# Causal attention on one core: row maxima moved for both row groups at once, first pass six steps ahead, another order for GpSimd's stack lay-out

## The chip, the cores and the metric

The kernel runs on one core of a Trainium2 chip. Its time is the device time of one execution, in microseconds (us), the median of several runs. The core's engines are TensorE (PE in the profile, PEld for its weight loads), VectorE (DVE), ScalarE (ACT), GpSimd (POOL) and SyncE (SP), which here does nothing but issue DMAs.

## What is computed

The input x is 16 sequences of 1024 tokens by 256 features. Four layers follow each other, each as x = x + layer(layernorm(x)): a state-space layer, a feed-forward coupling network, attention, and the coupling network once more. The change is in the attention layer alone:

```python
x_proj = x @ Wqkv + bqkv
q = x_proj[:, :, :C].reshape(B, n_head, T, hd)
k = x_proj[:, :, C:2 * C].reshape(B, n_head, T, hd)
v = x_proj[:, :, 2 * C:].reshape(B, n_head, T, hd)
att = jnp.einsum('bhtd,bhsd->bhts', q, k) * (1.0 / jnp.sqrt(jnp.float32(hd)))
causal = jnp.tril(jnp.ones((T, T), dtype=bool))
att = jnp.where(causal, att, jnp.float32(-jnp.inf))
att = jax.nn.softmax(att, axis=-1)
y = att @ v
y = jnp.transpose(y, (0, 2, 1, 3)).reshape(B, T, C)
return y @ Wproj + bproj
```

Here B = 16, T = 1024, C = 256, n_head = 16 and hd = 16. The reshape has no transpose: head h is 64 neighbouring tokens, each of which holds 16 positions of that head. So a head has 1024 positions of 16 features, and there are 16 sequences x 16 heads.

## The kernel before

The attention phase takes the 16 sequences in turns b = 0..15. A turn has four slots q = 0..3, one for each group of four heads (a quad; quad number 4b + q). A slot has 20 steps (STEPS = 2 * UNITS2, UNITS2 = 10). In each step TensorE computes two things for two different quads, interleaved block by block:

- The second pass of the slot's own quad (second_piece, L1980, with its mask product L1928): scores key by query, with the row maxima subtracted inside the product. For this a 49th row of the query stack holds each query's maximum. ScalarE takes exp of the scores (exponentiate, L1839), and times_v (L2008) multiplies them by the values, at every odd step.
- The first pass of a later quad (first_piece, L1958): the plain scores, of which VectorE takes the row maxima (maxima, L1719 with the causal mask added, L1722 without). A quad has UNITS1 = 18 units of first pass, nine for each half p of the queries (PASS1). Units 1 and 8 of nine are one masked piece of 512 columns, units 3, 5 and 7 are two masked pieces (384 + 128, 256 + 256, 128 + 384), the others one plain piece of 512.

Both passes work on two row groups g (partitions 0 to 63 and 64 to 127): in a block, the second pass uses group g and the first pass group 1 - g, so that the two products run side by side in the array. A block below is one such pair; a step has two blocks. The first pass writes into three PSUM banks in rotation (first_wait, semaphore s1_free): a block may start when VectorE has finished with what the third-last first-pass block wrote. The second pass has three banks likewise (second_wait, exp_done).

The first pass runs LEAD = 4 steps ahead (first_pass_at): in a slot, steps 0 to 13 do units 4 to 17 of the next quad, steps 14 and 15 have no first pass, and steps 16 to 19 do units 0 to 3 of the quad after it. The prologue does all 18 units of quad 0 and LEAD units of quad 1.

When a half's nine units are done (step 4 for p = 0, step 13 for p = 1), VectorE reduces the maxima to row_max (L1727), waits on max_moved for the buffer, and transposes them into row_max_T (L1733). SyncE then moves them with eight small DMAs (move_max, L1417) into the 49th row of the query stack: tasks at steps 6 and 15 of its slot. TensorE waits for the moves of half p at step p of the next slot (L1970).

Beside the two passes, one side task on TensorE stands at every even step from 2 to 16 (x_events): finished heads turned back (L2050), the output turned and projected (L2057, L2065), and the input of a later half sequence turned (L2032) and projected to q and k (L2036) and to v (L2042). Each uses the one bank x_ps. In slot 3, the two turned pieces of x ("project" 0 and 1) come at PE steps 4 and 8 and the first projection of them at step 10. Between them stand a copy by ScalarE (project, L1849) and a split into a high and a low part by GpSimd (split, L1541 and L1543); TensorE waits for the second split (split_done) before the projection at step 10.

GpSimd also lays out the stacks of quad + 3: lay_out (L1553, L1555) copies each of the two staged tiles, queries and keys, into its stack in two pieces, at task times LAY_OUT_AT = 6.3, 7.6, 10.2, 12.2. The first piece of a side waits for its staged loads (L1397, twelve DMAs of 128 KB, issued at a slot's start).

Every engine runs its tasks in the order of these step numbers (in_order sorts them, ties in the order in which they were added).

## Time and profile before

| | |
|---|---|
| median of 3 runs | 3927.08 us (3926.39 to 3935.58) |
| span of the profiled execution | 3930.1 us |
| PE busy, share of the span | 3667.3 us, 93% |
| DVE busy | 2960.1 us, 75% |
| ACT busy | 2237.0 us, 57% |
| POOL busy | 1663.9 us, 42% |
| the four steady slots of one turn (1923.9 to 2063.9) | 140.0 us |

The profile lists no device time of its own for the profiled execution; its span, from first to last instruction, is 3.0 us above the median and inside the range of the runs. Attention's steps begin near 1077 us and end near 3303 us; what stands before and after them are the other three layers.

The span is cut by time (windows), by who waited for whom (waits), and by single instructions (timeline). A row of the timeline gives start, duration, engine, line, operation, output and inputs, shapes, how many were merged, and in brackets the idle time of the engine before it and what ended it. SyncE's rows are the time in which it issued.

### The profile page before, as it was taken

How to read it: one execution, taken by the hardware profiler on the slowest of the kernel's cores; microseconds unless marked ns; L12 is line 12 of the kernel's file. 1: busy time of each engine (PE TensorE's matmuls, PEld its weight loads, DVE VectorE, ACT ScalarE, POOL GpSimd, SP SyncE). 2: the span in 40 equal slices, each digit the busy share in tenths (PEclk: the TensorE clock that was granted, in tenths of full speed). 3: DMA queues.
4: the chain of work that ended last, by engine and by line, in shares of the span. 5: the costliest groups of instructions: out<-in, count | busy, mean ns of one | idle time of the engine just before them, and what ended most of it. 6: DMA issues, size and time to landing. Idle time of an engine off the chain costs nothing. (4 is left out here: it accounts for less than half of the span.)

```text
span 3930.1 us, 77952 instructions
## 1 busy us (share of the span) xinstructions
PE 3667.3 (93%) x26062; PEld 2353.8 (60%) x26062; DVE 2960.1 (75%) x9275; ACT 2237.0 (57%) x4407; POOL 1663.9 (42%) x2027
## 2 busy tenths in 40 slices
PE   6998999998689999999999999999999997999997
...
GB/s 71 102 101 103 43 65 65 46 57 35 158 112 114 112 117 107 121 109 115 123 108 116 117 112 118 105 126 104 117 122 110 101 71 61 34 69 60 65 39 49
DMA packets 701469, 361.31 MB, mean 92 GB/s; under 512 B 305072, under 2 KB 668080, under 8 KB 701104
## 3 DMA queue, kind: packets, MB, share of 16 engines
q1 hardware_dynamic: 701104, 356.65, 50.8%
...
## 5 line engine op out<-in xcount | busy, mean ns | idle before, releaser
L1839 ACT ACTIVATE att_probs<-att_s 128x512 f32<-128x512 f32 (+1 forms) x2560 | 1319.3, 557 | 755.3 <-PE att_s L1928 430.9
L1719 DVE CUSTOM_DVE_ANT_0 att_s<-att_s,att_above 128x384 f32<-128x384 f32 (+3 forms) x2048 | 958.0, 514 | 189.0 <-PE att_s L1958 188.9
L1980 PE MATMUL att_s<-att_qs,att_ks 49*128 49x512 f32 (+3 forms) x3072 | 917.9, 388 | 90.0 <-ACT att_probs L1839 29.1
L1958 PE MATMUL att_s<-att_ks,att_qs 48*128 48x512 f32 (+3 forms) x3072 | 964.2, 407 | 5.8 <-DVE att_maxima L1722 3.7
L1980 PEld LDWEIGHTS att_s<-att_qs,att_ks 49*128 49x128 f32 x3072 | 459.7, 185 | 650.9 <-ACT att_probs L1839 433.6
L1722 DVE TENSOR_REDUCE att_maxima<-att_s 128x1 f32<-128x512 f32 x1024 | 668.8, 682 | 225.6 <-PE att_s L1958 219.3
L2008 PE MATMUL att_o_ps<-att_probs,att_vs 128*32 128x512 f32 (+3 forms) x6144 | 632.1, 499 | 0.5 <-ACT att_probs L1839 0.5
L1958 PEld LDWEIGHTS att_s<-att_ks,att_qs 48*128 48x128 f32 x3072 | 487.6, 188 | 25.1 <-DVE att_maxima L1719 8.0
L1097 PE MATMUL ffn_h2p<-ffn_h,ffn_w 128*128 128x512 f32 x768 | 363.3, 595 | 3.0 <-ACT ffn_h L968 0.9
L1928 PE MATMUL att_s<-att_mask,att_places 64*128 64x64 bf16 (+1 forms) x3072 | 332.5, 205 | 0.0
L1719 DVE DVE_READ_ACCUMULATOR2_ANT att_maxima<- 128x1 f32 x2048 | 290.0, 142 | 0.0
L946 ACT ACTIVATE ffn_uv<-ffn_uvp 128x512 f32<-128x512 f32 x256 | 153.1, 598 | 238.1 <-PE ffn_uvp L1072 238.1
L1612 POOL TENSOR_TENSOR att_x_res<-att_x_res,att_bp_row 128x512 f32<-128x512 f32 x60 | 76.2, 1285 | 420.6 <-DMA att_x_res<-x 419.7
L1555 POOL CAST att_qs<-att_staged 113x1024 fp32r<-113x1024 f32 x128 | 251.9, 1991 | 0.0
L976 ACT ACTIVATE ffn_h<-ffn_turned,ffn_b 128x512 f32<-128x512 f32 x384 | 241.9, 683 | 13.5 <-PE ffn_turned L1088 11.6
L1555 POOL CAST att_ks<-att_staged 113x1024 fp32r<-113x1024 f32 x126 | 249.4, 1992 | 0.0
L968 ACT ACTIVATE ffn_h<-ffn_h2p,ffn_b 128x512 f32<-128x512 f32 x192 | 131.9, 687 | 196.1 <-PE ffn_h2p L1097 196.1
L2008 PEld LDWEIGHTS att_o_ps<-att_probs,att_vs 128*32 128x32 f32 x6144 | 134.2, 108 | 161.1 <-issue 121.7
L1088 PEld LDWEIGHTS ffn_turned<-identf,ffn_uv 128*128 128x128 f32 x1536 | 174.5, 142 | 75.6 <-issue 53.9
L2036 PE MATMUL att_x_ps<-att_xnT,att_wqkv 128*128 128x512 f32 x714 | 198.0, 413 | 17.5 <-POOL att_xnT L1543 17.5
L158 ACT ACTIVATE ssm_xnT<-ssm_turned 128x512 fp32r<-128x512 f32 x64 | 34.9, 595 | 313.2 <-PE ssm_turned L166 313.2
L1088 PE MATMUL ffn_turned<-identf,ffn_uv 128*128 128x128 f32 x1536 | 201.6, 274 | 10.3 <-DVE ffn_uv L823 8.0
...
## 6 DMA issues: line engine op xcount, KB each, us to landing
...
qk_scratch<-att_parts SPq DMA_DIRECT2D x128, 512.0 KB, 3.7
...
```

Source lines behind the costliest of these rows:

```text
L976: last = a(h1[k][:, f, :], turned_ps[:, f, :], ACT.Gelu, bias=b1[:, f:f + 1])
L1088: last = pe.transpose(turned_ps[:, f, t * P:(t + 1) * P], of[:, t, f * P:(f + 1) * P], identf[:, :])
L1097: last = mm(h2_ps[:, :], w2[:, f, :], h1[k][:, f, :], start=(f == 0), stop=(f == KT - 1))
L1555: last = g.tensor_copy(stack[0:ROWS, :].rearrange("p (t c) -> p t c", c=HD)[:, e * n:(e + 1) * n, :], staged[side][0:ROWS, :, e * n:(e + 1 ...
L1719: last = v.tensor_tensor_reduce(scores, scores, above[:, CH - w:CH], 1.0, -3.0e38, ALU.add, ALU.max, to)
L1722: last = v.tensor_reduce(to, scores, AX.X, ALU.max)
L1839: a(probs[u % 2][2 * g + p][:, 0:n], bank[:, 0:n], ACT.Exp).then_inc(exp_done, 1)
L1928: last = mm(blocks[:, at, GROUP * half:GROUP * (half + 1)], places[rows, 2 * (1 - k) + half, :], mask[rows, 1 - k, 0:len(cols), :], start= ...
L1958: last = mm(bank[:, col:col + w], rows_of(qs[buf], g, KROWS, p, BT * blk, BT * (blk + 1)), rows_of(ks[buf], g, KROWS, p, t0, t1), start=k ...
L1980: last = mm(bank[:, col:col + w], rows_of(ks[buf], g, SHIFT + 1, p, BT * j, BT * (j + 1)), rows_of(qs[buf], g, SHIFT + 1, p, t0, t1), star ...
L2008: last = mm(o_ps[32 * i:32 * i + 32, HD * (t0 - first_t):HD * (t1 - first_t)], vs[s][:, NBLK * head + j, :], probs[u % 2][i][:, col:col + ...
L2036: last = mm(bank[:, :], wq[i][:, f, cols], xnT[k][:, f, :], start=(n == 0), stop=(n == KT * len(PARTS_R) - 1))
```

## The change

Three things change:

1. move_max issues four DMAs instead of eight: each takes the eight blocks of both row groups (16 partitions of row_max_T) and writes two partitions of the query stack, instead of 8 partitions into one. Bytes and the number of 128-byte pieces stay; the waits on max_moved count 64 instead of 128 for each quad. SyncE's two tasks stand at steps 4 and 13 instead of 6 and 15.
2. LEAD is 6 instead of 4. Steps 0 to 11 do units 6 to 17 of the next quad, steps 12 and 13 have no first pass, steps 14 to 19 do units 0 to 5 of the quad after it. The row maxima are reduced at steps 2 and 11 instead of 4 and 13. The prologue does six units of quad 1 instead of four.
3. In slot 3 alone, GpSimd's lay-out tasks stand at 9.2, 9.4, 11.2 and 13.2 instead of 6.3, 7.6, 10.2 and 12.2.

```diff
--- before.py
+++ after.py
@@ -1221,9 +1221,10 @@
     FIRST_U2, LAST_U2 = (0, 3), (2, 9)
     UNITS1, UNITS2 = 2 * len(PASS1), len(PASS2)
     STEPS = 2 * UNITS2
-    LEAD = 4
+    LEAD = 6
     EVACUATE_AT = (7, 1)
-    LAY_OUT_AT, PREPARE_AT, PIECES = (6.3, 7.6, 10.2, 12.2), 6, 2
+    LAY_OUT_AT, LAY_OUT_BEHIND_X_AT = (6.3, 7.6, 10.2, 12.2), (9.2, 9.4, 11.2, 13.2)
+    PREPARE_AT, PIECES = 6, 2
     NORMALISE_AT = (14.4, 15.5, 16.5, 17.5)
 
     X_PROLOGUE = 22
@@ -1411,11 +1412,10 @@
 
                 def move_max(quad, buf, p):
                     sp.wait_ge(row_max_turned, 2 * quad + p + 1)
-                    for g in range(2):
-                        to = qs[buf][GROUP * g + SHIFT:GROUP * g + SHIFT + 1, NBLK * P * p:NBLK * P * (p + 1)].bitcast(F32)
-                        for a in range(4):
-                            sp.dma_start(to.rearrange("o (n a r) -> o n a r", a=4, r=32)[:, :, a, :],
-                                         row_max_T[p][32 * a + NBLK * g:32 * a + NBLK * (g + 1), :]).then_inc(max_moved[p], 16)
+                    to = qs[buf][SHIFT:SHIFT + GROUP + 1:GROUP, NBLK * P * p:NBLK * P * (p + 1)].bitcast(F32)
+                    for a in range(4):
+                        sp.dma_start(to.rearrange("g (n a r) -> g n a r", a=4, r=32)[:, :, a, :],
+                                     row_max_T[p][32 * a:32 * a + 2 * NBLK, :]).then_inc(max_moved[p], 16)
 
                 def load_res(b, r):
                     k = r % 2
@@ -1435,8 +1435,8 @@
                                            (4 * b + 5, 2 * b + 2, 0, 1), (4 * b + 6, 2 * b + 3, 1, 0))[q]
                         tasks += [(side, lambda side=side: load_stack(quad, hb, s, qq, side)) for side in range(2)]
                     if more or q < 3:
-                        tasks += [(6, lambda: move_max(4 * b + q + 1, (q + 1) % 4, 0)),
-                                  (15, lambda: move_max(4 * b + q + 1, (q + 1) % 4, 1))]
+                        tasks += [(4, lambda: move_max(4 * b + q + 1, (q + 1) % 4, 0)),
+                                  (13, lambda: move_max(4 * b + q + 1, (q + 1) % 4, 1))]
                     if q == 0:
                         if not first:
                             tasks += [(2, lambda r=r: load_res(b - 1, r)) for r in range(2)]
@@ -1630,7 +1630,7 @@
                     if more or q == 0:
                         for side in range(2):
                             for e in range(PIECES):
-                                tasks += [(LAY_OUT_AT[PIECES * side + e],
+                                tasks += [((LAY_OUT_BEHIND_X_AT if q == 3 else LAY_OUT_AT)[PIECES * side + e],
                                            lambda side=side, e=e: lay_out(quad + 3, side, e, not first or q > 0))]
                     in_order(tasks)
 
@@ -1728,7 +1728,7 @@
                                         maxima_of[p][:, :, :, :].rearrange("p g n e -> p (g n) e"),
                                         AX.X, ALU.max).then_inc(row_max_ready, 1)
                         if not isinstance(quad, int) or quad > 0:
-                            dve.wait_ge(max_moved[p], 128 * quad)
+                            dve.wait_ge(max_moved[p], 64 * quad)
                         dve.wait_ge(row_max_ready, 2 * quad + p + 1)
                         v.transpose(row_max_T[p][:, :], row_max[p][:, :].bitcast(F32)).then_inc(row_max_turned, 1)
 
@@ -1967,7 +1967,7 @@
                         before = 3 if use >= 3 else (1, 4, 4)[use]
                         pe.wait_ge(exp_done, 2 * STEPS * quad + 2 * step + g - before + 1)
                     if step < 2 and g == 0:
-                        pe.wait_ge(max_moved[step % 2], 128 * (quad + 1))
+                        pe.wait_ge(max_moved[step % 2], 64 * (quad + 1))
 
                 def second_piece(buf, step, g, k):
```

How this moves rows on three engines, where the prediction speaks of them:

VectorE in a slot 1, from the maxima of step 2 to the first unit behind the row maximum. RECIPROCAL and the TENSOR_TENSOR after it are the division of the turned heads; row_max is L1727. Before:

```order
L1722 TENSOR_REDUCE att_maxima0<-att_s1_0 128x1
L1722 TENSOR_REDUCE att_maxima0<-att_s1_1 128x1
L1741 RECIPROCAL att_recip<-att_x_ps 128x16
L1744 TENSOR_TENSOR att_y<-att_x_ps,att_recip 128x8x32
L1719 ISA att_s1_2,att_maxima0<-att_s1_2,att_above 128x128
L1719 ISA att_maxima0 128x1
...
L1719 ISA att_s1_2,att_maxima0<-att_s1_2,att_above 128x512
L1719 ISA att_maxima0 128x1
L1727 TENSOR_REDUCE att_row_max0<-att_maxima0 128x16
L1733 STREAM_TRANSPOSE att_row_max_T0<-att_row_max0 128x32
L1722 TENSOR_REDUCE att_maxima1<-att_s1_0 128x1
```

After:

```order
L1722 TENSOR_REDUCE att_maxima0<-att_s1_0 128x1
L1722 TENSOR_REDUCE att_maxima0<-att_s1_1 128x1
L1719 ISA att_s1_2,att_maxima0<-att_s1_2,att_above 128x128
L1719 ISA att_maxima0 128x1
...
L1719 ISA att_s1_2,att_maxima0<-att_s1_2,att_above 128x512
L1719 ISA att_maxima0 128x1
L1727 TENSOR_REDUCE att_row_max0<-att_maxima0 128x16
L1733 STREAM_TRANSPOSE att_row_max_T0<-att_row_max0 128x32
L1741 RECIPROCAL att_recip<-att_x_ps 128x16
L1744 TENSOR_TENSOR att_y<-att_x_ps,att_recip 128x8x32
L1722 TENSOR_REDUCE att_maxima1<-att_s1_0 128x1
```

The row maximum and its transpose come two units earlier, ahead of the division of the heads, and the plain unit that followed the division at step 4 now follows it at step 3.

GpSimd in a slot 3, from the split of the first turned piece on (full and xnT are the splits of the turned input, qs and ks the stacks, parts the splits of the projections). Before:

```order
L1541 CAST att_xnT0<-att_full0 128x512
L1543 TENSOR_TENSOR att_xnT1<-att_full0,att_xnT0 128x512
L1553 TENSOR_TENSOR att_pool_carrier<-att_eps 1x1
L1555 CAST att_qs2<-att_staged0 113x1024 x2
L1541 CAST att_xnT0<-att_full1 128x512
L1543 TENSOR_TENSOR att_xnT1<-att_full1,att_xnT0 128x512
L1553 TENSOR_TENSOR att_pool_carrier<-att_eps 1x1
L1555 CAST att_ks2<-att_staged1 113x1024
L1541 CAST att_parts<-att_full2 128x512
L1543 TENSOR_TENSOR att_parts<-att_full2,att_parts 128x512
L1555 CAST att_ks2<-att_staged1 113x1024
```

After:

```order
L1541 CAST att_xnT0<-att_full0 128x512
L1543 TENSOR_TENSOR att_xnT1<-att_full0,att_xnT0 128x512
L1541 CAST att_xnT0<-att_full1 128x512
L1543 TENSOR_TENSOR att_xnT1<-att_full1,att_xnT0 128x512
L1553 TENSOR_TENSOR att_pool_carrier<-att_eps 1x1
L1555 CAST att_qs2<-att_staged0 113x1024 x2
L1541 CAST att_parts<-att_full2 128x512
L1543 TENSOR_TENSOR att_parts<-att_full2,att_parts 128x512
L1553 TENSOR_TENSOR att_pool_carrier<-att_eps 1x1
L1555 CAST att_ks2<-att_staged1 113x1024
L1541 CAST att_parts<-att_full0 128x512
```

The second split of the turned input now stands directly behind the first, and each lay-out piece moved behind one more split.

TensorE at the end of a slot, second block of step 17 and both blocks of step 18 (s2 is the second pass, s1 the first). Before:

```order
L1980 MATMUL att_s2_1<-att_qs2,att_ks2 128x384
L1958 MATMUL att_s1_0<-att_ks0,att_qs0 128x512
L1980 MATMUL att_s2_1<-att_qs2,att_ks2 128x128
L1928 MATMUL att_s2_1<-att_mask,att_places 128x2x64 x2
L1980 MATMUL att_s2_2<-att_qs2,att_ks2 128x256
L1928 MATMUL att_s2_2<-att_mask,att_places 128x64 x2
L1958 MATMUL att_s1_1<-att_ks0,att_qs0 128x512
L1980 MATMUL att_s2_0<-att_qs2,att_ks2 128x256
L1928 MATMUL att_s2_0<-att_mask,att_places 128x64 x2
L1958 MATMUL att_s1_2<-att_ks0,att_qs0 128x512
```

After:

```order
L1980 MATMUL att_s2_1<-att_qs2,att_ks2 128x384
L1958 MATMUL att_s1_1<-att_ks0,att_qs0 128x384
L1980 MATMUL att_s2_1<-att_qs2,att_ks2 128x128
L1928 MATMUL att_s2_1<-att_mask,att_places 128x2x64 x2
L1958 MATMUL att_s1_1<-att_ks0,att_qs0 128x128
L1980 MATMUL att_s2_2<-att_qs2,att_ks2 128x256
L1928 MATMUL att_s2_2<-att_mask,att_places 128x64 x2
L1958 MATMUL att_s1_2<-att_ks0,att_qs0 128x512
L1980 MATMUL att_s2_0<-att_qs2,att_ks2 128x256
L1928 MATMUL att_s2_0<-att_mask,att_places 128x64 x2
L1958 MATMUL att_s1_0<-att_ks0,att_qs0 128x512
```

The block in which the first pass had one piece of 512 columns now has two, 384 and 128, with the second behind the masks of the other pass.

## Rows read from the trace of the kernel before

**Rows 1.** The page's third part, DMA: packets, MB, share of 16 engines.

```profile
q1 hardware_dynamic: 701104, 356.65, 50.8%
```

**Rows 2.** Windows: length; PE, PEld, DVE, ACT, POOL busy (instructions); clock; DMA share; GB/s.

```profile
1923.90:2063.90 140.00, 134.31 (x1156) 78.41 (x1155) 111.97 (x374) 93.85 (x189) 77.12 (x68) 1.00 0.76 114
1958.80:1991.10 32.30, 31.58 (x284) 18.24 (x282) 27.57 (x91) 22.73 (x47) 14.45 (x12) 1.00 0.63 84
```

**Rows 3.** Waits of PE, 1100 to 3230: us in total, times, longest us.

```profile
PE att_s L1980 <- ACT att_probs L1839: 25.5, 65, 0.4
PE att_s L1980 <- DVE att_maxima L1722: 24.9, 35, 1.1
PE att_x_ps L2036 <- POOL att_xnT L1543: 17.5, 14, 1.8
PE att_s L1980 <- DVE att_maxima L1719: 16.0, 49, 0.3
```

**Rows 4.** Timeline of two slots 3: ScalarE's copy, GpSimd's second split, the projection.

```profile
1760.90 0.60 ACT L1849 ACTIVATE att_full<-att_x_ps 128x512 f32<-128x512 f32 x1
1762.37 0.60 POOL L1541 CAST att_xnT<-att_full 128x512 fp32r<-128x512 f32 x1
1764.46 0.71 PE L2036 MATMUL att_x_ps<-att_xnT,att_wqkv 128*128 128x512 f32 x2 [1.79 <-POOL att_xnT L1543]
...
2041.37 0.61 ACT L1849 ACTIVATE att_full<-att_x_ps 128x512 f32<-128x512 f32 x1
2042.04 0.61 POOL L1541 CAST att_xnT<-att_full 128x512 fp32r<-128x512 f32 x1
2042.73 1.27 POOL L1543 TENSOR_TENSOR att_xnT<-att_full,att_xnT 128x512 fp32r<-128x512 f32 x1
2044.14 1.61 PE L2036 MATMUL att_x_ps<-att_xnT,att_wqkv 128*128 128x512 f32 x6 [1.02 <-POOL att_xnT L1543]
```

**Rows 5.** Timeline of SP and PE at the first steps, and two windows there.

```profile
1058.36 5.59 SPq L1417 DMA_DIRECT2D att_qs<-att_row_max_T  x8
1064.05 5.96 SPq L1397 DMA_DIRECT2D att_staged<-qk_scratch  x12
1076.50 6.43 SPq L1417 DMA_DIRECT2D att_qs<-att_row_max_T  x8
1088.29 0.79 PE L1980 MATMUL att_s<-att_qs,att_ks 49*128 49x512 f32 x1 [10.02 <-DMA att_qs<-att_row_max_T]
1058.00:1064.00 6.00, 4.39 (x12) 1.87 (x11) 4.58 (x12) 1.97 (x2) 0.00 (x0) 0.78 0.01 1
1064.00:1087.00 23.00, 13.96 (x34) 7.48 (x33) 15.14 (x53) 1.19 (x2) 7.82 (x6) 0.50 1.15 191
```

**Rows 6.** Waits of PE, 3230 to 3303, the one on a move.

```profile
PE att_s L1980 <- DMA att_qs<-att_row_max_T: 0.7, 1, 0.7
```

**Rows 7.** Timeline of DVE and PE at the end of a slot 1.

```profile
1987.79 0.70 DVE L1719 CUSTOM_DVE_ANT_0 att_s<-att_s,att_above 128x512 f32<-128x512 f32 x1 [0.49 <-PE att_s L1958]
1988.70 0.35 PE L1980 MATMUL att_s<-att_qs,att_ks 49*128 49x256 f32 x1 [0.33 <-DVE att_maxima L1719]
1990.68 0.57 DVE L1719 CUSTOM_DVE_ANT_0 att_s<-att_s,att_above 128x384 f32<-128x384 f32 x1 [0.21 <-PE att_s L1958]
1991.70 0.47 PE L1980 MATMUL att_s<-att_qs,att_ks 49*128 49x512 f32 x1 [0.39 <-ACT att_probs L1839]
```

**Rows 8.** Timeline of DVE in a slot 1, steps 3 to 5, and PE's first block of step 5.

```profile
1963.70 0.29 DVE L1719 CUSTOM_DVE_ANT_0 att_s<-att_s,att_above 128x128 f32<-128x128 f32 x1
1965.21 0.73 DVE L1719 CUSTOM_DVE_ANT_0 att_s<-att_s,att_above 128x512 f32<-128x512 f32 x1
1967.11 1.25 DVE L1722 TENSOR_REDUCE att_maxima<-att_s 128x1 f32<-128x512 f32 x2
1965.56 0.29 PE L1980 MATMUL att_s<-att_qs,att_ks 49*128 49x256 f32 x1
```

**Rows 9.** Window with a lowered clock near the end of attention.

```profile
3190.00:3203.70 13.70, 13.70 (x50) 6.94 (x50) 6.31 (x25) 4.97 (x10) 10.35 (x8) 0.50 0.68 76
```

## The prediction

> **What bounds the kernel now.** I read the windows first, then TensorE's waits, then the timeline around each wait. In a steady turn of 140.0 us TensorE is busy 134.31 us, VectorE 111.97 and ScalarE 93.85, at the full clock [rows 2]. So TensorE sets the pace, and a change pays only where it shortens one of its idle pieces. They are few: from 1100 to 3230 it waits 25.5 us for ScalarE, 24.9 and 16.0 us for VectorE's maxima and 17.5 us for GpSimd's split, 83.9 us in all [rows 3]. No wait for a moved row maximum is among them; such waits stand only at the two ends, 10.02 us in the first slot and 0.7 us in the last [rows 5, 6]. VectorE is the second to watch: in a slot 1 it is busy 27.57 of 32.30 us [rows 2], and nearly all of its idle time falls where there is no first pass.
>
> **Part 1, the order on GpSimd.** The wait for the split occurs once in a turn, in slot 3. At 2042.04 the split starts 0.06 us after the end of ScalarE's copy (2041.37 + 0.61 = 2041.98), and yet TensorE waits 1.02 us [rows 4]: the wait is made of the copy's time and of the split's own 0.61 and 1.27 us, and no order on GpSimd shortens that. At 1762.37 the copy had ended at 1761.50, the lay-out held GpSimd for 0.87 us, and TensorE waited 1.79 us [rows 4]. So what the new order can give is the part over 1.02 us: 17.5 - 14 x 1.02 = 3.2 us over the 14 waits [rows 3, 4]. It costs nothing: what is laid out late is first read a slot later, and the later splits have two full steps each.
>
> **Part 2, the row maxima in four DMAs.** SyncE issues eight in 5.59 us [rows 5]; four should take half. In steady slots no one waits for them: worth nothing. In the prologue they stand on the path. SyncE issues the first half's moves from 1058.36, then the loads of quad 2's stacks from 1064.05, then stores, then the second half's moves from 1076.50, and TensorE resumes at 1088.29. From 1058 to 1064 the DMA engines are at 0.01 of their time, from 1064 to 1087 they are full [rows 5]. So the end of the queue is set by when the heavy transfers start, and this is earlier by half of 5.59: 2.8 us. TensorE would in that case resume at 1085.5. The two added units of quad 1 run inside this wait: at VectorE's 1.25 us for a plain unit [rows 8], and somewhat more for a masked one, they take some 3 us of the 10.02. The last slot's 0.7 us [rows 6] goes as well, since its moves start two steps earlier and are shorter, and the two units that the loop no longer holds save about 0.6 us at the end (estimate: two steps of unpaired blocks beside two of paired ones). Sum: 4.1 us, all gain; from below zero gain if the queue is full anyway, to 5.6 us if both moves count.
>
> The Trainium skill, DMA: Bandwidth & Descriptors, section "Why a DMA increments its semaphore by 16 and not by 1", says that a DMA from SP's queue runs on as many engines as divide the slowest dimensions of both its sides, 16 at most. The old moves (8 partitions to one of 8 blocks) would run on 8 engines, the new ones (16 partitions to two) on 2, with 32 pieces each instead of 8. The rule speaks against the change; no view here shows a packet's engine. At the mean packet time of the page, 0.508 x 3930.1 x 16 / 701104 = 0.046 us [rows 1], it would make 1.1 us more until a move has landed, as an estimate, and the prologue's gain would be 1.7 instead of 2.8 us.
>
> **Part 3, LEAD 6.** The work is the same; what changes is which first-pass unit stands beside which step. Two places matter.
>
> *End of a slot.* Steps 18 and 0 have no side task, so blocks follow each other with nothing between them, and the block at step 19 must wait for VectorE's maximum of the block at the end of step 17, three blocks back. Before, this is one masked piece of 512: VectorE starts at 1987.79 and TensorE resumes at 1988.70, 0.91 us on, after an idle 0.33 [rows 7]. It now becomes unit 3, pieces of 384 and 128, as the one at 1990.68, from which TensorE resumes at 1991.70, 1.02 us on [rows 7]: 0.11 us more. Besides, its second piece is issued behind the other pass's piece of 128 and its masks, where the single 512 was issued first; this costs between 0 and 0.14 us more, and I take the middle, 0.07. So 0.18 us in each of 61 slots: 11.0 us (6.7 to 15.3). The wait at step 1 (0.39 us, put down to ScalarE, but VectorE's unit ends 0.15 us before it) keeps its size, since 256 + 256 takes VectorE as long as 384 + 128.
>
> *Start of a slot.* The masked unit 8 and the row maximum move from step 4 to step 2, where a plain unit stood. From 1965.21 to 1967.11 they take 1.90 us, a plain unit 1.25 [rows 8]. So VectorE is 0.65 us further behind at step 3, and the division of the heads now follows this too. Before, unit 7 starts at 1963.70 in a slot 1; now unit 9 starts near 1964.4, its second half ends near 1965.73, and TensorE's first block of step 5, which stood at 1965.56 [rows 8], must wait for it and some 0.14 us of signalling (the distance from VectorE's end to TensorE's start, as 0.15 at 1991.70), to 1965.87: 0.3 us. From then the two orders have given VectorE the same work. Slots 1 and 3 (small side tasks at steps 2 and 4) pay this: 30 x 0.28 = 8.4 us. In slots 0 and 2 the side task of step 4 is the long one, and VectorE recovers before it matters: 0.05 x 31 = 1.6 us. The bounds for both together are 0 and 0.65 x 30 = 19.5 us.
>
> *Pairing.* The unpaired steps 12 and 13 carry no masks of the second pass, 14 and 15 did; the masks now run beside a first-pass block. I take 0.05 us gained per slot, 3 us (0 to 6).
>
> **Sum.** On the profiled execution's 3930.1 us: -3.2 - 4.1 + 11.0 + 8.4 + 1.6 - 3.0 = +10.7 us. The median of the runs lies 3.0 us below this span, so 3927.1 + 10.7 = 3937.8 us; I say 3937.
>
> **Rivals.**
>
> *The longer waits for VectorE do not come (A, chance 0.20).* If the block at step 19 and the ones at step 5 wait no longer than before, only -3.2 - 4.1 and half of the pairing, -1.5, remain: 3927.1 - 8.8 = 3918. For it: VectorE has idle time before step 17's maximum (0.49 us before 1987.79 [rows 7]). Against it: the wait there is latency, not backlog, and VectorE's idle time does not shorten it.
>
> *The whole wait for GpSimd goes (B, chance 0.13).* If the changed phases also bring ScalarE's copy 1 us ahead of TensorE, all 17.5 us go, with 4.1 and 3: 3927.1 - 24.6 = 3902.5. Against it: the split starts 0.06 us behind the copy in the undisturbed case [rows 4], and nothing moves the copy.
>
> *VectorE becomes the bound (C, chance 0.22), slower.* Its price is the whole of the moved row maximum in slots 1 and 3, 19.5 us, and the upper end at step 19, 15.3 us: with 1.6, and less 3.2, 4.1 and 3.0, +26.1, which is 3953. It decides from the point where VectorE's backlog at step 4 exceeds the slack of three banks; by the rows it exceeds it by 0.3 us in slots 1 and 3, and C holds if nothing of it is recovered.
>
> *The clock (D, chance 0.07).* From 3190.00 to 3203.70 TensorE had only 0.50 of its clock while busy throughout [rows 9]; half of 13.7 us, 6.9 us, is lost there, and it could go or come a second time with another arrangement near the end: 3930 or 3944 about the forecast.
>
> *The moves are hidden anyway.* For the steady slots this is my forecast, and if the queue in the prologue is full regardless, 2.8 us less gain gives 3940; it is part of the forecast's own range.
>
> **How the numbers follow.** The forecast itself has a chance of 0.38, with a range of its own from 3930 to 3945. The bound of what a measurement can tell is 0.3%, 11.8 us: faster is below 3915.3, slower above 3938.9. Faster: B whole and 0.04 of A, 0.17. Slower: C whole, 0.11 of the forecast and 0.02 of D, 0.35. The rest, 0.48, is within. The range from 3908 to 3955 holds the forecast, A, D, the upper third of B and, since its middle lies at 3953, somewhat over half of C; it leaves out 0.18.
>
> **What would show each step.** Right: the wait on the split counts 15 or 14 times with 1.0 us each, longest about 1.1; the first slot's wait on the moves ends near 1085.5, and no move is waited for in the last; the idle before step 19's first block reads about 0.5 instead of 0.33 in every slot; a new wait of 0.2 to 0.3 us for VectorE's maxima at step 5 in slots 1 and 3; a turn of four slots of about 141 us instead of 140.0. Wrong: a turn of under 139.6 us, which would say that the first pass further ahead gave TensorE time that I don't see; waits on moved maxima in steady slots, if four DMAs land later than eight; or the idle before step 19 unchanged at 0.33.

## The result, and the profile after

The changed kernel takes 3964.91 us (median, 3954.92 to 3968.43) against 3928.19 us of the kernel before in the same comparison (3926.39 to 3937.59). The ratio is 1.008, with a 95% interval from 1.0066 to 1.0094: slower by 31 us by the ratio and 37 by the medians. The prediction said 3937 us and at most 3955.

First the page's line on DMA and two windows of the kernel after, a steady turn and its slot 1 (columns as in [rows 2]):

```profile
q1 hardware_dynamic: 693936, 356.62, 50.0%
...
1932.60:2074.15 141.55, 134.66 (x1156) 79.19 (x1155) 112.78 (x374) 94.00 (x189) 77.02 (x68) 1.00 0.74 113
1967.87:2000.66 32.79, 31.67 (x283) 18.39 (x282) 27.77 (x91) 22.76 (x48) 14.39 (x12) 1.00 0.83 104
```

The turn is 1.55 us longer than in [rows 2], with the same instructions on every engine and the clock at 1.00. That is the steady loss. TensorE's waits from 1100 to 3266 (us in total, times, longest) answer to [rows 3]:

```profile
PE att_s L1980 <- DVE att_maxima L1719: 33.0, 63, 0.6
PE att_s L1980 <- ACT att_probs L1839: 28.6, 67, 0.5
PE att_s L1980 <- DVE att_maxima L1722: 27.2, 35, 1.1
PE att_x_ps L2036 <- POOL att_xnT L1543: 13.2, 14, 0.9
PE att_s L1928 <- issue: 2.9, 2, 2.5
PE att_s L1980 <- issue: 1.6, 1, 1.6
```

The wait for masked maxima (L1719) has doubled, from 16.0 to 33.0 us. The wait for GpSimd's split has fallen from 17.5 to 13.2 us, and is 0.9 us each time. The last two rows are waits put down to "issue": TensorE had nothing it waited for, and its next instruction came late. The kernel before has one such wait in this stretch, 1.4 us, at full clock; the changed kernel has four, of 1.6, 2.5, 0.6 and 0.4 us (the row of the one of 0.6 us is not shown). Where the two long ones stand is seen in the timeline. The windows of lowered clock are below them; the first and the third come with these two waits, the second does not:

```profile
1720.33 0.44 PE L1980 MATMUL att_s<-att_qs,att_ks 49*128 49x384 f32 x1 [1.59 <-issue]
2581.54 0.21 PE L1928 MATMUL att_s<-att_mask,att_places 64*128 64x64 bf16 x1 [2.54 <-issue]
...
1720.70:1724.20 3.50, 3.50 (x15) 2.17 (x11) 1.45 (x3) 0.87 (x2) 0.00 (x0) 0.51 1.51 110
2499.00:2512.60 13.60, 13.60 (x80) 9.08 (x78) 7.57 (x24) 5.37 (x11) 0.00 (x0) 0.50 1.23 126
2580.90:2587.70 6.80, 6.16 (x28) 3.53 (x31) 2.06 (x5) 1.62 (x4) 0.72 (x2) 0.50 1.04 81
```

In each of the three windows TensorE has 0.50 of its clock (the level of 1.2 GHz) while busy nearly throughout. The kernel before had none between 1097.6 and 3159.3.

What such an instruction waited for is most likely its own fetching. The third part of the page has a DMA queue for instructions (here of the kernel before: packets, MB, share of 16 engines):

```profile
q8 instruction: 204, 3.34, 0.4%
```

These are packets of 16 KB. In all 17 profiles together TensorE has 25 waits of over 1 us put down to issue between 1100 and 3300, and each of the 25 ends 1.2 to 2.0 us after the end of such a packet, of which one comes only about every 14.6 us.

The prologue and the first slot answer to [rows 5], the end of a slot 1 to [rows 7]:

```profile
1057.44 2.33 SPq L1417 DMA_DIRECT2D att_qs<-att_row_max_T  x4
1059.87 5.74 SPq L1398 DMA_DIRECT2D att_staged<-qk_scratch  x12
1072.42 2.15 SPq L1417 DMA_DIRECT2D att_qs<-att_row_max_T  x4
1081.97 0.79 PE L1980 MATMUL att_s<-att_qs,att_ks 49*128 49x512 f32 x1 [1.51 <-DMA att_qs<-att_row_max_T]
...
1997.34 0.57 DVE L1719 CUSTOM_DVE_ANT_0 att_s<-att_s,att_above 128x384 f32<-128x384 f32 x1 [0.54 <-PE att_s L1958]
1997.82 0.33 DVE L1719 CUSTOM_DVE_ANT_0 att_s<-att_s,att_above 128x128 f32<-128x128 f32 x1
1998.36 0.35 PE L1980 MATMUL att_s<-att_qs,att_ks 49*128 49x256 f32 x1 [0.61 <-DVE att_maxima L1719]
```

TensorE waits 1.51 us for the moves instead of 10.02 us, in part because it comes to this wait later: VectorE and TensorE do two more units ahead of the loop. At step 19 it waits 0.61 instead of 0.33 us.

**Where the 36.2 us between the two profiled spans lie.** I cut attention into turns, from the start of the first exponential of a turn to that of the next. Before, turn 0 begins at 1077.6 and turn 1 at 1223.9; after, at 1079.8 and 1220.5: -3.4 us. Turns 1 to 13 take 1819.8 before and 1857.8 after: +38.1. The last two take 258.9 and 260.1: +1.2. The rest gives +0.3. The shortest turn, which nothing disturbs, is 139.65 before and 141.55 after, so 13 x 1.90 = 24.7 us of the 38.1 are steady. What turns 1 to 13 take beyond 13 times the shortest was 4.3 us and is now 17.6: 13.3 us for late instructions and lowered clock.

Where in a turn the steady part lies, I read from the starts of TensorE's blocks of the second pass, counted from the first one of their slot (medians over turns 2 to 12, us more than in the kernel before):

| stretch | slot 0 | slot 1 | slot 2 | slot 3 | a turn |
|---|---|---|---|---|---|
| steps 0 to 5 | 0.04 | 0.30 | 0.02 | 0.30 | 0.66 |
| steps 6 to 11 | 0.25 | 0.08 | 0.28 | 0.06 | 0.67 |
| steps 12 to 16 | -0.12 | -0.12 | -0.15 | -0.14 | -0.53 |
| steps 17 and 18 | 0.12 | 0.01 | 0.00 | 0.01 | 0.14 |
| the wait at step 19 | 0.15 | 0.28 | 0.27 | 0.27 | 0.97 |

The second run of the changed kernel (e17) and LEAD 6 alone (e1) give the same sums to within 0.05. The whole kernels are compared by the two numbers above, the shortest turn and what turns 1 to 13 take beyond it:

| kernel | shortest turn | turns 1 to 13 beyond 13 of these | at half clock, 1100 to 3240 | time against before |
|---|---|---|---|---|
| before | 139.65 | 4.3 | 17.1 | |
| changed | 141.55 | 17.6 | 30.7 | 1.0080 |
| changed, second run (e17) | 141.56 | 13.9 | 13.7 | 1.0097 |
| LEAD 6 alone (e1) | 141.54 | 12.7 | 30.7 | 1.0093 |
| all but LEAD (e2) | 139.60 | 5.9 | 6.8 | 0.9979 |
| order on GpSimd alone (e6) | 139.60 | 3.0 | 0.0 | 0.9977 |
| four DMAs alone (e15) | 139.67 | 13.3 | 13.6 | 0.9998 |
| changed, row maximum later (e4) | 140.90 | 21.8 | 37.5 | 1.0091 |
| changed, plain unit at 17 (e16) | 140.03 | 12.7 | 27.3 | 1.0001 |
| changed, both (e9) | 139.56 | 4.2 | 6.8 | 0.9996 |
| changed, plain at odd places (e3) | 141.16 | 46.1 | 105.9 | 1.0136 |
| LEAD 5 (e11) | 141.55 | 42.9 | 81.9 | 1.0126 |
| before, plain at odd places (e5) | 140.67 | 11.8 | 6.9 | 1.0098 |
| same with the other two parts (e7) | 140.62 | 17.1 | 34.1 | 1.0064 |
| before, copy of 192 (e10) | 140.30 | 8.7 | 6.8 | 1.0024 |
| before, copy of 320 (e12) | 140.63 | 7.5 | 23.8 | 1.0031 |
| LEAD 4, plain at 17 (e13) | 139.54 | 5.4 | 6.8 | 0.9977 |

### The profile page after: what moved, and what is told of

It reads as the page before. It is cut to its first block and busy times, and to the rows that moved or that the text cites. A ratio compares the mean times of both kernels' runs of the same rounds, so it can differ in the third digit from the quotient of the medians.

```text
span 3966.3 us, 77436 instructions
## 1 busy us (share of the span) xinstructions
PE 3689.6 (93%) x26062; PEld 2373.5 (60%) x26062; DVE 2972.0 (75%) x9275; ACT 2241.4 (57%) x4407; POOL 1663.0 (42%) x2027
## 5 line engine op out<-in xcount | busy, mean ns | idle before, releaser
L1719 DVE CUSTOM_DVE_ANT_0 att_s<-att_s,att_above 128x384 f32<-128x384 f32 (+3 forms) x2048 | 958.4, 516 | 156.2 <-PE att_s L1958 154.1
L1980 PE MATMUL att_s<-att_qs,att_ks 49*128 49x512 f32 (+3 forms) x3072 | 928.9, 391 | 106.5 <-DVE att_maxima L1719 34.0
L1958 PE MATMUL att_s<-att_ks,att_qs 48*128 48x512 f32 (+3 forms) x3072 | 990.4, 410 | 6.7 <-DVE att_maxima L1722 4.4
L1980 PEld LDWEIGHTS att_s<-att_qs,att_ks 49*128 49x128 f32 x3072 | 470.3, 186 | 675.9 <-ACT att_probs L1839 435.8
L1722 DVE TENSOR_REDUCE att_maxima<-att_s 128x1 f32<-128x512 f32 x1024 | 677.9, 685 | 258.4 <-PE att_s L1958 256.0
L1928 PE MATMUL att_s<-att_mask,att_places 64*128 64x64 bf16 (+1 forms) x3072 | 361.2, 206 | 2.9 <-issue 2.9
L1719 DVE DVE_READ_ACCUMULATOR2_ANT att_maxima<- 128x1 f32 x2048 | 290.7, 142 | 0.0
L2036 PE MATMUL att_x_ps<-att_xnT,att_wqkv 128*128 128x512 f32 x714 | 200.6, 417 | 13.8 <-POOL att_xnT L1543 13.2
```

Source lines behind the costliest of these rows:

```text
L1719: last = v.tensor_tensor_reduce(scores, scores, above[:, CH - w:CH], 1.0, -3.0e38, ALU.add, ALU.max, to)
L1722: last = v.tensor_reduce(to, scores, AX.X, ALU.max)
L1928: last = mm(blocks[:, at, GROUP * half:GROUP * (half + 1)], places[rows, 2 * (1 - k) + half, :], mask[rows, 1 - k, 0:len(cols), :], start= ...
L1958: last = mm(bank[:, col:col + w], rows_of(qs[buf], g, KROWS, p, BT * blk, BT * (blk + 1)), rows_of(ks[buf], g, KROWS, p, t0, t1), start=k ...
L1980: last = mm(bank[:, col:col + w], rows_of(ks[buf], g, SHIFT + 1, p, BT * j, BT * (j + 1)), rows_of(qs[buf], g, SHIFT + 1, p, t0, t1), star ...
L2036: last = mm(bank[:, :], wq[i][:, f, cols], xnT[k][:, f, :], start=(n == 0), stop=(n == KT * len(PARTS_R) - 1))
```

## The experiments

### Which part loses: LEAD alone, and everything but LEAD

```diff
-    LEAD = 4
+    LEAD = 6
```

> The kernel before with LEAD 6 and nothing else (eight moves of a row maximum, at steps 6 and 15; the old order on GpSimd). Theory T: the loss comes from the first pass being six slots ahead, which makes TensorE wait longer for VectorE at step 19 and at steps 4 and 5 (in the profiles 0.61 instead of 0.33 us a slot, and 0.35 us in slots 1 and 3), and it brings the stretches at the lower clock too. Then this kernel loses as much as the changed one and does not get the gains of the other two parts: about 3965 + 3 (layout) + 3 to 5 (moves) = 3968 to 3975 us, TensorE's wait for the maxima about 33 us in all from 1080 to 3270. Rival U: the pairing makes only the steady 20 us or so, and the other half of the loss, the short stretches at half clock with their idle pieces ahead, belongs to the moves in four DMAs or to the new order on GpSimd. Then this kernel stands at 3945 to 3955 us and its profile shows the clock at 1.00 from 1100 to 3150.

Measured: 3969.71 us, ratio 1.0093 (1.0077 to 1.011). Its waits from 1100 to 3266:

```profile
PE att_s L1980 <- DVE att_maxima L1719: 32.9, 63, 0.6
PE att_s L1980 <- ACT att_probs L1839: 28.7, 67, 0.5
PE att_s L1980 <- DVE att_maxima L1722: 26.8, 36, 1.1
```

These are the changed kernel's, and so are the shortest turn and the half clock. Theory T holds: LEAD makes the whole loss, and the two other parts were not needed for the stretches at half clock.

The counterpart is the changed kernel with

```diff
-    LEAD = 6
+    LEAD = 4
-                        tasks += [(4, lambda: move_max(4 * b + q + 1, (q + 1) % 4, 0)),
-                                  (13, lambda: move_max(4 * b + q + 1, (q + 1) % 4, 1))]
+                        tasks += [(6, lambda: move_max(4 * b + q + 1, (q + 1) % 4, 0)),
+                                  (15, lambda: move_max(4 * b + q + 1, (q + 1) % 4, 1))]
```

> The changed kernel with LEAD back at 4 and the moves back at steps 6 and 15: what remains of the change is the order on GpSimd and four DMAs instead of eight. Theory T: -3.2 us from the waits for the split (14 at 0.94 to 1.02 us instead of 17.5 us in all) and -3 to -5 us from the prologue and the end: 3920 to 3924 us, no stretch of half clock that the kernel before does not have. Rival U (these two parts bring the stretches at half clock): 3930 to 3945 us.

Measured: 3921.58 us against 3932.07, ratio 0.9979 (0.9968 to 0.9989). The other two parts together gain some 8 us, as T said. Against T, the profile has a stretch of 6.8 us at half clock (at 1854.7) where the kernel before has none; it follows an instruction that came 2.4 us late.

### The two small parts by themselves

The order on GpSimd alone (LAY_OUT_BEHIND_X_AT in the kernel before):

> The kernel before with the new order on GpSimd and nothing else. Theory T: the 14 waits for the split of slot 3 fall from 17.5 us in all to 14 x 1.0 us and nothing else changes: 3 us less than before, 3924 to 3930 us, the slot 3 at 35.7 us in every turn instead of 35.7 to 36.5. Rival U (this part has a cost of its own elsewhere on GpSimd's queue): the same waits, but the time at or above that of before.

Measured: 3913.80 us against 3922.82, ratio 0.9977 (0.9967 to 0.9987). All ten runs lie between 3912.97 and 3916.12; those of before are spread from 3915.10 to 3932.67. The wait it was made for reads

```profile
PE att_x_ps L2037 <- POOL att_xnT L1544: 14.2, 14, 1.0
```

and has lost 3.3 us, as expected. The time has lost 9 us. What part of the rest may be is seen in the kernels that keep the old order. In the one with four DMAs alone, two of TensorE's waits for the split reach 2.3 us, and the clock is at half behind each:

```profile
1337.38 2.90 PE L2035 MATMUL att_x_ps<-att_xnT,att_wqkv 128*128 128x512 f32 x6 [2.30 <-POOL att_xnT L1542]
2599.73 1.64 PE L2035 MATMUL att_x_ps<-att_xnT,att_wqkv 128*128 128x512 f32 x4 [2.35 <-POOL att_xnT L1542]
...
1337.30:1340.70 3.40, 3.32 (x9) 2.32 (x11) 0.00 (x0) 0.00 (x0) 2.01 (x2) 0.50 0.00 0
2600.20:2603.60 3.40, 3.40 (x14) 1.92 (x17) 0.58 (x3) 0.62 (x2) 1.45 (x1) 0.50 0.00 0
```

Each of these slots is 2.8 us longer than its like (38.5 instead of 35.72 us), 1.3 us by the longer wait and the rest by the clock. In the four kernels run with the old order and LEAD 4 there are nine waits for the split of 2.0 to 2.4 us, and five have half clock behind them (the profile of the kernel before itself has none above 1.8 us); in the kernels with the new order the longest is 1.1 us, and none has. The two stretches of [rows 9] and at 3159.3, 17.1 us in all, are gone as well in this one profile: the last two turns take 252.0 instead of 258.9 us. That the new order caused this is not shown, since the waits ahead of them (0.67 and 0.66 us) are there with full clock too. Nor is the narrow spread explained: it did not come with the same order in the kernels with four DMAs (3912.78 to 3931.45 and 3903.22 to 3922.92).

Four DMAs instead of eight, alone:

> The kernel before with a row maximum's moves in four DMAs instead of eight and nothing else. Theory T: 3 to 6 us less, all of it ahead of the first slot and in it, as the wait on the moves there falls from 10.0 to about 4 us; a steady turn as before. Rival (the moves land later when each is one transfer of twice as many pieces, or SyncE was not what held the stacks up): within 1 us of before, or slower.

Measured: 3919.95 us against 3919.25, ratio 0.9998 (0.9984 to 1.0012). In the profile the gain is there:

```profile
1053.97 2.34 SPq L1416 DMA_DIRECT2D att_qs<-att_row_max_T  x4
1069.12 2.87 SPq L1416 DMA_DIRECT2D att_qs<-att_row_max_T  x4
1079.56 0.79 PE L1979 MATMUL att_s<-att_qs,att_ks 49*128 49x512 f32 x1 [5.09 <-DMA att_qs<-att_row_max_T]
```

The wait on the moves is 5.09 instead of 10.02 us and turn 0 takes 142.38 instead of 146.27 us, so 3.9 us as theory T had it; the interval of the times, -6 to +5 us, is too wide to show it. The time from SyncE's last issue to TensorE's start is 1079.56 - 1071.99 = 7.6 us, where it was 1088.29 - 1082.93 = 5.4 us [rows 5], so some of what SyncE saves in issuing (12.0 us of issuing before, 5.2 now) is waited for all the same. By the rule that the Trainium skill, DMA: Bandwidth & Descriptors, gives in its section "Why a DMA increments its semaphore by 16 and not by 1", the new moves run on 2 engines instead of 8. The 2.2 us are of the sign that this gives and twice the 1.1 us that the prediction estimated from it, but they may as well be the stores ahead of them in the queue; no run here tells the two apart.

### What at LEAD 6 costs: the two-piece units and the row maximum

The changed kernel with two of the first pass's units changed about, so that step 17 has a plain unit (one piece of 512, no masks) in place of 384 + 128. PASS1 holds for both halves of the queries, so the same exchange also puts a plain unit at step 6, where the second half has its 384 + 128:

```diff
-    PASS1 = [[(7, 0, 32)], [(7, 32, 64)], [(6, 0, 32)], [(6, 32, 56), (0, 0, 8)], [(5, 0, 32)],
+    PASS1 = [[(7, 0, 32)], [(7, 32, 64)], [(6, 32, 56), (0, 0, 8)], [(6, 0, 32)], [(5, 0, 32)],
              [(5, 32, 48), (1, 0, 16)], [(4, 0, 32)], [(4, 32, 40), (2, 0, 24)], [(3, 0, 32)]]
```

> The changed kernel with only the two units changed about that put a plain one at step 17 (the row maximum stays at step 2). Steady part, from the run with both edits (turn 139.6 us) and the one with the later row maximum alone (141.0): the unit is worth 1.3 us a turn, the turn here 140.25 us. Theory T (the half-clock stretches of the changed kernel come where the wait of 0.6 us and the next of 0.42 us stand close together, at the ends of slot 3, and with the missing instructions in slot 2): none at the ends of slot 3, 3928 to 3940 us. Rival V (they come with LEAD 6 and the later row maximum removed them by chance): 20 us or more of half clock between 1100 and 3240 us, 3940 to 3955 us.

Measured: 3930.34 us against 3929.49, ratio 1.0001 (0.9986 to 1.0015). Waits from 1100 to 3230:

```profile
PE att_s L1980 <- ACT att_probs L1839: 41.1, 112, 0.9
PE att_s L1980 <- DVE att_maxima L1722: 26.2, 35, 1.1
PE att_x_ps L2036 <- POOL att_xnT L1543: 15.1, 14, 1.1
PE att_x_ps L2036 <- issue: 1.9, 1, 1.9
```

The row for L1719 has gone; ScalarE ends the wait at step 19 now:

```profile
1990.63 0.35 PE L1980 MATMUL att_s<-att_qs,att_ks 49*128 49x256 f32 x1 [0.27 <-ACT att_probs L1839]
```

The turn falls from 141.55 to 140.03 us. By the stretches of the table above, 1.22 us of this come at step 19, where the wait is now below that of the kernel before (0.27 instead of 0.33 us), and 0.45 us in steps 6 to 11; the others lose 0.12. Nearly all of the loss in the time is gone with this one exchange. Against rival V the time is 39.6 us below that of the changed kernel on the same chip (3969.90); but V is right that 20 us or more of half clock stay (27.3 us), none of it at the ends of slots 3. Of the 39 us between the two spans (3966.8 and 3927.8), 1.52 x 13 = 19.8 us lie in turns 1 to 13 as their steady part, some 8 us in the last two turns (260.0 to 251.9), 6.1 us ahead of attention's steps and 5.5 us behind them, where the two kernels are the same. So by the profiles 1.52 x 15 = 23 us are the exchange's steady part, and nothing here ties the rest to it.

The other suspect, the row maximum one unit later:

```diff
-                    if unit % len(PASS1) == len(PASS1) - 1:
+                    if unit in (len(PASS1), UNITS1 - 1):
+                        p = unit // len(PASS1) if unit == UNITS1 - 1 else 0
```

> The changed kernel, where VectorE reduces the row maximum of the first row group one unit later (behind the unit of step 3 instead of step 2), so that step 2 carries 0.65 us less of VectorE's work. Theory T (the wait at steps 4 and 5 in slots 1 and 3 is VectorE's backlog from this reduction at step 2): the wait goes where it is only a matter of order, 0.2 to 0.35 us in 30 slots, 6 to 10 us: 3955 to 3959 us. Rival U: the backlog is the sum of units 8 and 9 with the division of the heads, wherever the reduction stands: the time is 3963 to 3968 us and the steps 4 and 5 take as long as in the changed kernel.

Measured: 3964.25 us, ratio 1.0091 (1.0062 to 1.012). In the time, no gain; in the profile, exactly the expected one. A steady slot 1 takes 32.49 instead of 32.79 us, and from the first to the second block of step 5 it is 0.34 instead of 0.58 us (the changed kernel's two rows first, then this kernel's):

```profile
1974.35 0.38 PE L1980 MATMUL att_s<-att_qs,att_ks 49*128 49x256 f32 x1
1974.93 0.35 PE L1980 MATMUL att_s<-att_qs,att_ks 49*128 49x256 f32 x1
```

```profile
1978.58:2011.07 32.49, 31.45 (x283) 18.32 (x281) 27.71 (x91) 22.77 (x47) 14.45 (x12) 1.00 0.81 102
...
1985.12 0.38 PE L1981 MATMUL att_s<-att_qs,att_ks 49*128 49x256 f32 x1
1985.46 0.28 PE L1981 MATMUL att_s<-att_qs,att_ks 49*128 49x256 f32 x1
```

The shortest turn is 0.65 us less; over 13 turns 8.5 us. They were given back: the first slot waits 5.4 us for the moves (1.5 in the changed kernel's profile), and turns 1 to 13 hold 4.2 us more of late instructions and half clock than the changed kernel. Both edits together:

> The changed kernel with only two of the first pass's units per row group changed about, so that a plain unit of one piece of 512 stands at step 17, while steps 8 and 19 keep theirs, and with the first row maximum one unit later. Theory T (steady part: the two-piece unit at step 17 makes the 0.61 us wait at step 19; and what is left over the kernel before is the lower clock that follows such waits): the wait at step 19 falls to about 0.3 us, slots 1 and 3 lose another 0.3 us (as the run with the later row maximum alone showed, 32.81 to 32.48 us), the turn comes to about 140.1 us, the pair of waits 0.6 and 0.42 us at the end of slot 3 is gone and no 13.6 us stretch of half clock follows there: 3930 to 3942 us. Rival V (the pairing costs elsewhere, or the stretches at half clock come with LEAD 6 whatever stands at step 17): 3950 to 3970 us.

Measured: 3922.03 us against 3922.82, ratio 0.9996 (0.9985 to 1.0007). The turn is

```profile
1922.10:2061.66 139.56, 133.81 (x1155) 78.29 (x1155) 112.68 (x374) 94.24 (x188) 76.94 (x68) 1.00 0.75 115
```

that of the kernel before in its best turns, with the first pass six slots ahead. So the distance costs nothing by itself: 1.52 us of each turn's 1.99 go with the exchanged units (step 19 and steps 6 to 11), 0.47 with the place of the row maximum (0.65 where the other edit is not there). Theory T expected 140.1 us for the turn: it had not counted that the exchange also helps in steps 6 to 11 and leaves a shorter wait at step 19 than the kernel before has.

### The same exchange carried further, and LEAD 5

First I had changed about more than that: in the changed kernel, plain one-piece units at all odd places.

```diff
-    PASS1 = [[(7, 0, 32)], [(7, 32, 64)], [(6, 0, 32)], [(6, 32, 56), (0, 0, 8)], [(5, 0, 32)],
-             [(5, 32, 48), (1, 0, 16)], [(4, 0, 32)], [(4, 32, 40), (2, 0, 24)], [(3, 0, 32)]]
+    PASS1 = [[(7, 32, 64)], [(7, 0, 32)], [(6, 32, 56), (0, 0, 8)], [(6, 0, 32)], [(5, 32, 48), (1, 0, 16)],
+             [(5, 0, 32)], [(4, 32, 40), (2, 0, 24)], [(4, 0, 32)], [(3, 0, 32)]]
```

> The changed kernel with the units of each row group of the first pass in another order: the plain one-piece unit and its two-piece neighbour change places, so that at step 17 a plain unit of one piece of 512 stands where 384 + 128 stood, at 19 likewise, and step 16 and 18 carry the two-piece ones. The work is the same. Theory T (the wait at step 19 is made by the unit whose maxima VectorE takes there): the idle before step 19 falls from 0.61 to 0.33 us or less in each of 61 slots, 17 us or more, and the other steps change by a few us in either direction: 3940 to 3950 us. Rival U (the pairing is minor): within 5 us of the changed kernel's 3965.

Measured: 3987.82 us, ratio 1.0136 (1.0087 to 1.0186). Both theories missed. The wait at step 19 fell to 0.27 us, but this order also puts a masked two-piece unit at step 7, where VectorE is already behind with the statistics of x, and TensorE waits for its maxima at the second block of step 8 and the first of step 9 in slots 0 and 2. Two rows and the window behind them:

```profile
2390.41 0.47 PE L1980 MATMUL att_s<-att_qs,att_ks 49*128 49x512 f32 x1 [0.98 <-DVE att_maxima L1719]
2391.17 0.46 PE L1980 MATMUL att_s<-att_qs,att_ks 49*128 49x512 f32 x1 [0.26 <-DVE att_maxima L1719]
...
2392.10:2398.90 6.80, 6.80 (x31) 2.60 (x24) 3.62 (x13) 3.09 (x6) 6.80 (x7) 0.50 0.89 125
```

Of 27 such pairs, 15 are followed by 3.4 to 10.2 us at half clock; the slot of the pair shown takes 3.0 us more than its like (38.7 instead of 35.75). In the kernel before and in the changed one, the same place has waits of mostly 0.80 to 0.85 and 0.1 us, and, between 1100 and 3200, no half clock behind them. LEAD 5, with the moves at 5 and 14 and the old order of the units, meets the same at step 7:

> The changed kernel with LEAD 5 instead of 6, and the moves one step later, at 5 and 14. At step 17 stands unit 2, plain, in one piece of 512, and the row maximum comes at step 3. Theory T (what costs is the unit at step 17 and the row maximum at step 2, not the distance as such): the wait at step 19 is 0.33 us or less, slots 1 and 3 lose little at steps 4 and 5, the turn is 139.5 to 140.5 us: 3915 to 3935 us. Rival V (the distance itself costs, each slot of lead about half of what six cost over four): 3940 to 3950 us.

Measured: 3973.71 us against 3922.82, ratio 1.0126 (1.0105 to 1.0146). The wait at step 19 is 0.12 to 0.17 us, as T said, but the time is far above both of the forecast ranges and the worst but one: 0.97 and 0.26 us at step 8, eight times followed by half clock, and besides a new wait of 8.9 us in all for the additions of the residual (L1752), which at step 12 now stand beside the last unit and the second row maximum. At a slot's end it gains, in its middle it loses.

Is it LEAD after all? The same order of units at LEAD 4, first on the kernel before, then with the other two parts:

> The kernel before (LEAD 4, old layout, eight moves) with the units of the first pass changed about in the same way as in the run of the changed kernel that became slower: plain one-piece units at the odd places, so that a plain unit stands at step 8 too. Theory T (what costs is which unit stands at step 8 and at step 17, not the distance of the two passes): the wait behind step 8 rises from about 0.95 to 1.25 us in slots 0 and 2, stretches of 3.4 to 10.3 us at half clock follow it in a third of the cases or more, and the time is 3945 to 3990 us although the wait at step 19 is gone. Rival W (half clock comes with a first pass further ahead than four): no such stretches, 3910 to 3925 us.

> LEAD 4, new order on GpSimd, four DMAs, and plain one-piece units at all odd places, so that one stands at step 8. The waits there read 0.95 to 1.0 and 0.26 us in slots 0 and 2; the steady turn is 140.6 us, about 1.0 us above that of the kernel with only the unit at step 17 changed. Theory T (at LEAD 4 these waits only cost themselves; what the same order lost on the kernel before beyond its turns came from the long waits for GpSimd): 3922 to 3935 us. Rival U (the waits at step 8 lower the clock in some executions at LEAD 4 as well): 3940 to 3960 us.

Measured: 3956.82 us against 3919.25, ratio 1.0098 (1.0067 to 1.013), and 3955.29 us against 3929.49, ratio 1.0064 (1.004 to 1.0087). So T's time was right for the first, though not the half clock that it expected, and rival U's for the second. The unit at step 7 costs at LEAD 4 as well: 1.0 us a turn by its waits (140.67 and 140.62 instead of 139.6), 15 us of the 25 to 37. In the second kernel 2 such pairs of waits (0.94 and 0.26 us) are followed by 10 us at half clock, in the first none in the one profile, which was its fastest run (3939.24 of 3939.24 to 3965.49). So the lowered clock follows nearly the same pair of waits in 15, 8, 2 and 0 cases of some 27 at LEAD 6, 5, 4 and 4, each counted in one profile.

### A longer wait at step 19 without LEAD 6

To separate the wait from the order, I put a copy by VectorE between the arrival of step 17's last block and its maximum, in the kernel before:

```diff
                         dve.wait_ge(s1_full, n + 2 - g)
+                        if g == 0 and unit == 1 and (not isinstance(quad, int) or quad > 0):
+                            v.tensor_copy(delay[:, :], above[:, 0:192])
```

> The kernel before with one added operation of VectorE in each slot, a copy of 128 x 192 between the arrival of the last block of step 17 and its maximum: its order, its moves and its units are as before, and only the latency for which the block at step 19 waits grows by the copy, some 0.2 to 0.3 us. Theory T (a longer wait at this place costs its own length, and brings stretches at half clock behind it): the wait at step 19 reads about 0.55 to 0.65 us, the steady turn is 0.8 to 1.2 us longer, and one to three stretches of 3.4 to 13.6 us at half clock appear between 1100 and 3150: 3945 to 3965 us. Rival W (the lower clock has to do with LEAD 6 otherwise): the turn longer by as much, the clock at 1.00 from 1100 to 3150: 3940 to 3946 us.

> As the run with the added copy of VectorE in each slot of the kernel before, with 128 x 320 instead of 128 x 192 (0.26 us there): about 0.39 us. The wait at step 19 should read 0.60 to 0.65 us, as in the changed kernel. Theory T (a wait as long as this, followed by the 0.42 us one at the end of slot 3, lets the clock fall there in some turns): one to three stretches of 13 us at half clock at the ends of slots 3, steady turn 140.8 us: 3945 to 3960 us. Rival W (waits only cost themselves): the turn 1.2 us longer over 15 turns, 3938 to 3945 us, and full clock from 1100 to 3150.

Measured: 3931.52 us against 3922.82, ratio 1.0024 (1.0012 to 1.0035), and 3933.49 us against 3919.25, ratio 1.0031 (1.0016 to 1.0045). The wider copy reproduces the waits of the changed kernel at the end of a slot 3:

```profile
2063.67 0.35 PE L1983 MATMUL att_s<-att_qs,att_ks 49*128 49x256 f32 x1 [0.58 <-DVE att_maxima L1722]
2066.04 0.50 PE L1983 MATMUL att_s<-att_qs,att_ks 49*128 49x512 f32 x1 [0.42 <-ACT att_probs L1842]
...
2061.00:2080.00 19.00, 18.00 (x187) 11.72 (x186) 17.10 (x58) 13.18 (x28) 1.88 (x2) 1.00 1.12 168
```

and the clock stays at 1.00 there. This is rival W's case: the waits cost their own length, 1.0 us in a turn of 140.63 and 15 us in all (W's times, 3940 to 3946 and 3938 to 3945 us, were too high, in part because the kernel before is 5 to 9 us faster in these comparisons than in the first). With the narrower copy there is one stretch of 3.4 us at half clock, behind an instruction that came 2.6 us late. Where the kernel with the wider copy has half clock between 1100 and 3150, it stands behind waits of 2.0 and 1.4 us for GpSimd. The two waits alone are thus not enough for the 13.6 us at 2499.

### The changed kernel again, and a version below both

> The changed kernel itself once more. Its steady turn is 141.6 us again. Theory T (the clock and the missing instructions are a matter of the single execution, with a mean that belongs to the kernel): again 20 to 40 us of half clock between 1100 and 3240 us, at other turns than before, and 3955 to 3970 us. Rival (the places belong to the kernel): the same turns 4, 9 and 10.

Measured: 3969.90 us against 3929.49, ratio 1.0097 (1.0075 to 1.012). The turn is 141.56 us again. The half clock is 13.7 us instead of 30.7, below the 20 us that theory T wanted at least, and in turns 13 and 15 instead of 4, 9, 10 and 15. The two longest of the late instructions, though, were late in the first profile as well: in turn 10 one of L1928 in slot 2 comes 2.25 us late (2.54 in the first profile), and in turn 13 one of L2036 comes 3.63 us late (0.63 in the first, and 1.5 to 3.4 us late in three other kernels with LEAD 5 or 6). So some places in the program are prone to it, and how late the instruction comes changes with the execution; the 1.59 us of turn 4 did not come again. Two profiles with 17 us between them in half clock differ by only 0.5 us in span (3966.3 and 3966.8), as other events fill in.

Last a candidate: LEAD 4, the new order on GpSimd, four DMAs, and a plain unit at step 17:

```diff
-    PASS1 = [[(7, 0, 32)], [(7, 32, 64)], [(6, 0, 32)], [(6, 32, 56), (0, 0, 8)], [(5, 0, 32)],
+    PASS1 = [[(7, 32, 64)], [(7, 0, 32)], [(6, 0, 32)], [(6, 32, 56), (0, 0, 8)], [(5, 0, 32)],
```

> A candidate: the new order on GpSimd and the four DMAs, LEAD 4, and the first two units of the first pass changed about, so that a plain unit instead of a masked one stands at step 17; steps 8 and 19 keep theirs. Theory T: the wait at step 19 falls from 0.33 to 0.27 us (put down to ScalarE), 0.06 x 61 = 4 us less than with four DMAs and the new order alone: 9 to 15 us below before. Rival: the masked unit, now at step 16, delays ScalarE or VectorE there by as much: 6 to 10 us below before.

Measured: 3914.43 us against 3919.25, ratio 0.9977 (0.9959 to 0.9994). It is below both kernels, but not below the new order on GpSimd alone, which has the same ratio. The shortest turn, 139.54 instead of 139.60, shows that the exchange is worth 0.06 us a turn at LEAD 4 where 4 us over the slots, 0.27 us a turn, were expected. The wait at step 19 did fall by 0.23 us a turn, but the wait for the split in slot 3 rose from 1.02 to 1.14 us.

## Why the prediction was wrong

- **The bound.** TensorE sets the pace and the turn grows with its waits: right in every kernel of the table.
- **"Two places matter."** This is the step that failed. There is a third: the unit of 384 + 128 stands in each half of the queries, so with LEAD 6 one comes to step 17 and another to step 6, where a masked unit of one piece stood. In steps 6 to 11 a turn loses 0.67 us, 10 us over all slots, for which the sum has no term. The exchange of the two units, which takes the 384 + 128 from step 6 as well, gives 0.45 us of the 0.67 back; what the other 0.22 are is open. A further 0.14 us a turn, 2 us, is lost in slot 0 just ahead of step 19.
- **End of a slot, +11.0 us (6.7 to 15.3).** Right in mechanism, at the upper end in size: the block at step 19 waits for unit 3's two pieces. From VectorE's start to TensorE's it is 1.02 us, as taken from [rows 7]; but the second piece and its masks delay VectorE's start, against the end of TensorE's work, by 0.17 us and not by 0.07 (the wait grew by 0.28 = 0.11 + 0.17, above my bound of 0.25). Slot 0 grew by 0.15 us only, so it is 0.97 us a turn and 15 us over the slots. The rows of the waits give 17.0 us, as the 0.14 us of slot 0 before are not counted in them.
- **Start of a slot, +8.4 and +1.6 us.** Right: 0.30 us in slots 1 and 3 and 0.66 us a turn, which is 10 us over the slots. It took the later row maximum to tie it to its cause, as no row of the waits names it.
- **Pairing, -3.0 us (0 to 6).** Right in sign, too small: from step 12 to step 16, where the unpaired steps lie, a turn gains 0.53 us, 8 us in all. So the five steady terms come to about 29 us where the forecast had 18.0.
- **Order on GpSimd, -3.2 us.** The waits fell by 3.3 us in its own run and 4.3 in the changed kernel. What I missed is that waits well beyond 1.0 us can be followed by half clock, and the last two turns were 7 us shorter; by its own run the part is worth 9 us, of which I can place 3.3 surely.
- **Moves, -4.1 us.** The gain is there, as large as forecast or a little larger, as both of the moves had stood in TensorE's way and not one. From SyncE's first issue to TensorE's start it is 29.9 us in the kernel before and in the one with LEAD 6 alone, and 24.5 us in the changed one (25.8 in its second run). Between the profiles turn 1 starts only 3.4 us earlier, and the difference is LEAD 6's: from the end of the wait to turn 1 it takes 138.5 us with LEAD 6, with or without the four DMAs, and 135.6 before. In the time of four DMAs alone the gain is not seen. No moved maximum is waited for in steady slots, as said.
- **What no term held: +13.3 us** in turns 1 to 13 for single late instructions and stretches at half clock (9.6 us by the second run of the changed kernel). Rival D had 6.9 us for one stretch near the end and a chance of 0.07; here it was four stretches, three of them where the kernel before had none. The forecast missed by 27 us: 11 us in the steady terms and 13.3 us here are most of it, and without either one the time would have stayed below 3955. C's 26.1 us lie near the steady loss, but by the wrong mechanism: the backlog cost in slots 1 and 3 what the forecast said, and the rest came from steps 6 to 11 and the longer wait at step 19.

The chance of 0.48 for "within 0.3%" came from the forecast's own middle, and with one place and the single events left out, that middle was 27 us too low.

What stays open is why half clock and long fetches are frequent in some kernels and rare in others. Neither the waits at step 19 nor LEAD alone bring them: in the runs with the added copy no half clock followed the waits at step 19, and LEAD 6 with both edits had 6.8 us. The changed kernel had 30.7 us in one profile and 13.7 in the other, where the kernel before had 17.1. Between kernels with the same order of units and long waits at step 8, LEAD 6 had the most (105.9 us against 34.1 and 6.9 at LEAD 4), and this is not explained.
